# A fused decoder layer: the last stage moved beside the last expert, the first expert rows in five loads, spare products in the last batch, and scatters behind the maxima's transfers

## What is computed

```python
gates = softmax(x_flat @ router_w + router_b)
_, topk_idx = top_k(gates, 2)
pos = cumsum(expert_mask, axis=0) - 1          # place of a row in its expert
buf[e, pos] = x_flat[row]                      # rows beyond the capacity are dropped
h = gelu(einsum('ecd,edh->ech', buf, w1) + b1)
out = einsum('ech,ehd->ecd', h, w2) + b2
y = sum over a row's experts of weight * out[expert, pos]
result = layernorm(x + y)
```

## Time and profile before

| | us |
|---|---|
| median of 3 runs | 2276.23 |
| lowest, highest | 2272.47, 2283.42 |
| the profiled execution, its own time | 2272.46 |
| its span | 2270.7 |
| PE busy in it | 2169.6 (96%) |
| DVE, ACT, Pool busy | 1180.0, 1007.8, 648.9 |

### The profile page before, as it was taken

How to read it: one execution, slowest core, us unless ns; L and a number is a source line. 1 busy time by engine, 2 the same in 40 slices (tenths; PEclk the granted TensorE clock), 3 DMA queues, 4 the chain that set the end, 5 groups by cost and what they waited for, 6 DMA issues and landing times. The chain is left out here.

```text
span 2270.7 us, 48602 instructions
## 1 busy us (share of the span) xinstructions
PE 2169.6 (96%) x18846; PEld 1509.7 (66%) x18846; DVE 1180.0 (52%) x2458; ACT 1007.8 (44%) x1538; POOL 648.9 (29%) x1001
## 2 busy tenths in 40 slices
PE   8999999999999999999999999999799999999990
PEld 4566666666666666666666666666478778787780
DVE  3466666766766766667676676764111111111114
ACT  1355555555555555555555555553231222212225
POOL 2112323333233332333323333222312122121223
PEclk6799999999999999999999999998799999999995
DMA  6301111111101111001010010100113331333217
GB/s 181 102 21 30 44 31 49 53 42 51 51 27 31 37 30 29 22 26 33 25 30 22 28 33 24 28 20 14 37 35 84 77 71 32 82 84 77 24 17 303
DMA packets 97667, 115.72 MB, mean 51 GB/s; under 512 B 12097, under 2 KB 91022, under 8 KB 95393
## 3 DMA queue, kind: packets, MB, share of 16 engines
q1 hardware_dynamic: 68112, 82.38, 11.5%
q0 software_dynamic: 17664, 18.35, 5.1%
q10 hardware_dynamic: 11664, 11.88, 1.8%
HBM read 64.53 MB, written 56.05 MB: 53 GB/s over the span
## 5 line engine op out<-in xcount | busy, mean ns | idle before, releaser
L867 DVE TENSOR_REDUCE smax<-ps_s 128x4 f32<-128x1024 f32 x500 | 610.0, 1220 | 352.3 <-PE ps_s L574 286.3
L753 ACT ACTIVATE prob<-ps_e 128x1024 f32<-128x1024 f32 x500 | 512.3, 1025 | 524.5 <-PE ps_e L583 427.4
L574 PE MATMUL ps_s<-stack 17*128 17x256 f32 x4000 | 574.1, 404 | 24.9 <-DVE smax L867 9.8
L583 PE MATMUL ps_e<-stack 18*128 18x256 f32 x4000 | 574.7, 405 | 5.6 <-DMA stack<-nrows 3.9
L574 PEld LDWEIGHTS ps_s<-stack 17*128 17x128 f32 x4000 | 350.6, 186 | 206.6 <-issue 97.7
L583 PEld LDWEIGHTS ps_e<-stack 18*128 18x128 f32 x4000 | 345.7, 186 | 11.4 <-DMA stack<-nrows 5.9
L1543 ACT ACTIVATE hid<-m_ps_h,b_sb 128x320 f32<-128x320 f32 x256 | 135.0, 527 | 415.7 <-PE m_ps_h L1503 411.5
L1503 PE MATMUL m_ps_h<-m_cols,w_sb 128*128 128x320 f32 x1024 | 293.3, 436 | 0.6 <-DVE m_cols L1560 0.6
L1520 PE MATMUL m_ps_o<-w_sb,hid 128*128 128x256 f32 x1280 | 278.9, 379 | 0.0
L1520 PEld LDWEIGHTS m_ps_o<-w_sb,hid 128*128 128x128 f32 x1280 | 243.2, 190 | 34.8
L599 PE MATMUL ps_w<-prob,val 128*32 128x256 f32 x4096 | 257.3, 393 | 1.3 <-ACT prob L753 1.3
(11 more groups left out here) (134 smaller groups left out, 2270.8 us busy)
## 6 DMA issues: line engine op xcount, KB each, us to landing
w_sb<-in_w SPq DMA_DIRECT2D x16, 1024.0 KB, 6.5
slot_rows_dram<-fill ACTq DMA_DIRECT2D x8, 1290.0 KB, 9.7
m_rows<-slot_rows_dram SPq DMA_DIRECT2D x16, 645.0 KB, 4.5
xT<-in_xT SPq DMA_DIRECT2D x32, 256.0 KB, 2.8
ctxT<-in_ctxT SPq DMA_DIRECT2D x32, 256.0 KB, 2.8
x_res<-in_x SPq DMA_DIRECT2D x32, 256.0 KB, 2.9
stack<-nrows SPq DMA_DIRECT2D x512, 2.0 KB
sums_dram<-x SPq DMA_DIRECT2D x32, 256.0 KB
```

What stands on the lines that cost most here:

```text
L574: mm = nc.tensor.matmul(scores[:, p % 2, t, :], stack[X][rows, Q, p // HG, t * P:(t + 1) * P], stack[X][rows, K, p // HG, :], start=True, ...
L583: mm = nc.tensor.matmul(shifted[:, p % 2, t, :], stack[Y][rows, K, h // HG, t * P:(t + 1) * P], stack[Y][rows, Q, h // HG, :], start=True, ...
L753: nc.scalar.activation(prob[:, h:h + 2, :].rearrange("p h s -> p (h s)"), shifted[:, :, :, :].rearrange("p h t s -> p (h t s)"), ACT.Exp, ...
L867: nc.vector.tensor_reduce(max_columns(X, p), scores[:, :, :, :], AX.X, ALU.max)\
```

## The change

Four parts.

1. *The last stage beside the last expert.* SP loads the eight groups of sums once the scatters of chunks 12 and 13 have landed. DVE, Pool and ACT work on the groups between their instructions for chunks 14 and 15: DVE all moments and the normalisation of groups 5 to 7, ACT the normalisation of groups 0 to 4 (22 of 40 tiles after the Gelus of chunk 14, two after each piece of chunk 15, four after the last). The last expert's results are no longer scattered into the sums. Pool gathers the sums of their rows (`l_got`, ten gathers), DVE adds them (`last_sum`), makes their moments and normalises them, and Pool scatters the finished rows over those that SP has written to the output, after all eight writes have landed.
2. *The first expert rows in five loads.* `m_rows` and `spin` are made before the first block (`FirstRows`); the tile `fill`, which held zeros in the first steps, now lies in `m_rows`. SP loads chunk 0 in five transfers, one per tile, at the end of the first block, as soon as it has seen the last scatters land. PE waits for each tile by itself.
3. *Spare products.* 8 in (32, CROSS), 14 in (33, SELF), 50 instead of 45 in (34, CROSS), and 4 at the start of the second block.
4. *Scatters.* In the SELF half step Pool waits for the four transfers of the first half of the maxima before it issues the scatters. For batch 30 the own positions and `place` come before the inverse deviation.

```diff
+            spins_beside_one_stream = {
+                (last + 1, CROSS): (0, (0, 0, 2, 3, 3, 0, 0, 0)), (last + 2, SELF): (2, (2, 2, 3, 2, 0, 2, 1, 2)),
+            }
...
-                     (last + 3, SELF, 3): 2, (last + 3, SELF, 7): 12, (last + 3, CROSS, 7): 45}
+                     (last + 3, SELF, 3): 2, (last + 3, SELF, 7): 12, (last + 3, CROSS, 7): 50}
...
+                    if (i, X) in spins_beside_one_stream:
+                        n, times = spins_beside_one_stream[i, X]
+                        if times[m] and n in held:
+                            steps_of, at_b, at_k = held[n]
+                            pe.wait_ge(steps_of.sem, steps_of.count(at_b, at_k))
+                        keep_warm(times[m], ps_w[:, n, :])
...
                     if there(i - 4) and i - 4 < NB - 2:
+                        if there(bX):
+                            pool.wait_ge(max_in[SELF].sem, max_in[SELF].count(bX, 64))
                         scatter(i - 4)
...
             sp.wait_ge(slots_zero, (E + 1) * 16)
+            sp.wait_ge(gone.sem, gone.count(NB - 1))
+            first_rows.load(sp)
...
+    def load(self, sp):
+        for c in range(CT):
+            sp.dma_start(self.rows[:, 0, c, :], DRAMS.slots[c * P:(c + 1) * P, :]).then_inc(self.come[c], 16)
...
         for u in range(2):
-            sp.wait_ge(sent.sems[u], sent.count(CHUNKS - 2 + u, u))
+            sp.wait_ge(sent.sems[u], sent.count(LAST - 2 + u, u))
...
+        for q in (0, 1, 2, 3, 5, 6, 4, 7):
+            if q < ACT_GROUPS:
+                sp.wait_ge(by_act.sem, by_act.count(q))
+            else:
+                sp.wait_ge(by_dve.sem, by_dve.count(q - ACT_GROUPS))
+            send_group(q)
...
+        fetch(0, 0, CT)
+        fetch(1, 0, 2)
+        group_inverse(0)
+        group_inverse(1)
+        fetch(1, 2, 4)
+        group_inverse(2)
+        fetch(1, 4, CT)
+        for q in range(3, GROUPS):
+            group_inverse(q)
+        last_inverse(0, 0, CT, 2 * CT, 0)
+        pool.wait_ge(c_sent, 16 * GROUPS)
+        place_last(0, 0, CT)
+        last_inverse(1, 0, CT - 1, 2 * (CT - 1), 0)
+        place_last(1, 0, 1)
+        last_inverse(1, CT - 1, CT, 2 * CT, 1)
+        place_last(1, 1, CT)
...
+                if q == CHUNKS - 1:
+                    for n in (22 + 2 * m, 23 + 2 * m):
+                        normalise(n // GT, n % GT)
+            if q == LAST:
+                for n in range(22):
+                    normalise(n // GT, n % GT)
...
+        group_moments(1, 0, GT)
+        group_moments(2, 0, GT // 2)
+        for c in range(CT):
+            last_sum(LAST, 0, last_pe, c)
+            q, part = divmod(5 + c, 2)
+            group_moments(q, part * GT // 2, (part + 1) * GT // 2)
+        for q in range(5, GROUPS):
+            group_moments(q, 0, GT)
+        last_moments(LAST, 0, 0, CT)
+        for q in range(ACT_GROUPS, GROUPS):
+            group_normalised(q)
+        last_normalised(0, 0, CT, 0)
+        dve.wait_ge(noted.sem, noted.count(LAST + 1))
+        for c in range(CT - 1):
+            last_sum(LAST + 1, 1, last_pe, c)
+        last_moments(LAST + 1, 1, 0, CT - 1)
+        last_sum(LAST + 1, 1, last_pe, CT - 1)
+        last_moments(LAST + 1, 1, CT - 1, CT)
+        last_normalised(1, 0, CT - 1, 0)
+        last_normalised(1, CT - 1, CT, 1)
```

More of the change, by code:

```diff
@@ L1456, in store, with fetch @@
                 ).then_inc(sent.sems[u], 16)
-        turns(pool, store)
+        def fetch(u, first, end):
+            if first == 0:
+                pool.wait_ge(noted.sem, noted.count(LAST + u))
+                pool.sem_inc(fence)
+            for c in range(first, end):
+                nc.gpsimd.indirect_dma_start(
+                    out=got[:, u, c, :], out_offset=None, in_=DRAMS.sums[:, :],
+                    in_offset=bass.IndirectOffsetOnAxis(ap=token_of[:, u, c:c + 1], axis=0),
+                    bounds_check=TOKENS + SPARE * P - 1, oob_is_err=False,
+                ).then_inc(fetched[u], 16)
@@ new lines, in last_inverse @@
+        def last_inverse(u, first, end, done, part):
+            pool.wait_ge(l_moments[u].sem, done)
+            pool.sem_inc(fences[0])
+            nc.gpsimd.tensor_scalar(l_veps[:, u, first:end], l_mv[:, u, first:end, 1], EPS, None, ALU.add)\
+              .then_inc(l_inv[u], 1)
+            pool.wait_ge(l_inv[u], 2 * part + 1)
+            pool.sem_inc(fences[0])
+            nc.gpsimd.tensor_tensor(l_rstd[:, u, first:end], l_veps[:, u, first:end], minus_half[:, 0:end - first],
+                                    ALU.pow).then_inc(l_inv[u], 1)
@@ L1532, in _, with normalise @@
     def _(act):
+        def normalise(q, g):
+            if g == 0:
+                act.wait_ge(inv, inverses(q, 4))
+            nc.scalar.activation(out_tile[:, q, g, :], out_tile[:, q, g, :], ACT.Identity, bias=shift[:, q, g:g + 1],
+                                 scale=rstd[:, q, g:g + 1]).then_inc(by_act.sem, 1)
         def emit(q, e, u, pe_):
@@ L1566, in columns, with group_moments @@
             nc.vector.tensor_copy(gate_of[:, u, :], rows[:, u, :, D + 1]).then_inc(noted.sem, 1)
+        def group_moments(q, first, end):
+            if first == 0:
+                dve.wait_ge(come[q], 16)
+            for g in range(first, end):
+                nc.vector.bn_stats(c_stats[:, q, g, :], out_tile[:, q, g, :]).then_inc(moments.sem, 1)
+            if end == GT:
+                dve.wait_ge(moments.sem, moments.count(q, GT))
+                dve.sem_inc(fences[1])
+                for g in range(GT):
+                    nc.vector.bn_aggr(mv[:, q, g, :], c_stats[:, q, g, :]).then_inc(moments.sem, 1)
@@ L1568, in emit, with last_normalised @@
+        def last_normalised(u, first, end, part):
+            dve.wait_ge(l_inv[u], 2 * part + 2)
+            for c in range(first, end):
+                nc.vector.tensor_scalar(res[:, u, c, :], res[:, u, c, :], l_mv[:, u, c, 0:1], l_rstd[:, u, c:c + 1],
+                                        ALU.subtract, ALU.mult).then_inc(l_normed[u], 1)
         def emit(q, e, u, pe_):
-            if not isinstance(q, int) or q + 1 < CHUNKS:
-                columns(q + 1, 1 - u)
+            columns(q + 1, 1 - u)
```

162 lines of the change are left out of this document (113 added, 49 removed).

## The result

The changed kernel takes **2250.3 us** (median of 4 runs, 2247.6 to 2253.6) against 2275.1 for the kernel before beside it: ratio 0.989, 95% interval 0.987 to 0.991. It is faster, but the gain is 25 us where 54 were forecast, and the time lies outside the range (2211 to 2238).

The account below looks back on a forecast made before the run. PE was taken as busy without a break at full clock except at the end, the last attention batch and the experts' start. 2272.5 - 37.2 - 6.2 - 8.9 = 2220.2, plus 2 for scatter: 2222 us, range 2211 to 2238.

Parts of the forecast that it names:

- Scatters behind the maxima: Steady attention loop, 28 batches: Pool waits for SP's four transfers before its four scatters; cost 0, gain 0.
- Cover 7.8 us: cost 0: Steady loop: scatters end at 1044.2 instead of 1038.6, still 7.8 us before Pool's addition at 1051.98, so nothing is lost.
- Slower: the new wait on Pool: Rival, steady loop: maxima over 7.8 us later than reckoned cost 1 us per further us in 28 batches; chance 0.03.
- if the period grows: Sign against the forecast, steady loop: a longer batch; Pool's addition was expected at the same place in an unchanged period.
- Last stage: End of the kernel: loads, moments, normalisations and sends move beside the last expert; -37.2 us (bounds -34 to -40).
- group 7's way to DRAM: Tail of the last stage: group 7 leaves DVE at 2206.8 and is in DRAM about 4 us later, 2210.9.
- Start of the experts: First expert rows: earlier load in five pieces (-3.4) and clock held by spares (-2.8); -6.2 us (bounds -0.5 to -6.5).
- The clock part: Start of the experts: if spares hold the clock, the first 24 hidden products take 6.46 instead of 9.27 us, -2.8.
- Spare products: Last batch of attention: 22 spares beside one stream hold the clock at 2.4 GHz; -8.9 us (bounds 0 or +4).
- the last four: Chances said to lie outside the range: tail shorter 0.06, stage not beside the expert 0.03, slower 0.03, gains eaten 0.02.
- the shorter tail: Rival, end of the kernel: plain placing lands in 2 us and DVE makes no wait; 2213 us, chance 0.06.
- both: Rival: clock not held and a last-expert queue in PE's way together; 2243 us, chance 0.05.

Follow-up runs that it names:

- e2: The kernel before with only Pool's wait for the maxima ahead of the scatters added; 2291.7 us, ratio 1.012 to the kernel before.
- e10: The changed kernel without Pool's wait for the maxima ahead of the scatters, run again on a chip with the pause; 2230.5 us, ratio 0.980 to the kernel before.
- e9: The changed kernel itself run once more, on a chip with the pause; 2250.3 us, ratio 0.989 to the kernel before.
- e18: The changed kernel without Pool's wait for the maxima, as the reference on e17's chip; 2229.6 us, ratio 0.980 to the kernel before.
- e16: The changed kernel without Pool's wait for the maxima, as the reference on the chip of e13 to e15; 2228.8 us, ratio 0.982 to the kernel before.
- e1: The changed kernel without Pool's wait for the maxima ahead of the scatters, all else as changed; 2222.6 us, ratio 0.980 to the kernel before.
- e4: e1 with the four scatters issued half a batch later, behind the additions of the turned parts; 2253.3 us, ratio 0.995 to the kernel before.
- e14: e1 with two of the four scatters of a batch issued, back to back; 2218.7 us, ratio 0.977 to the kernel before.
- e15: e1 with all four scatters, one each at four places of the batch; 2219.1 us, ratio 0.977 to the kernel before.
- e13: e1 with only the first of the four scatters of a batch issued; 2210.3 us, ratio 0.973 to the kernel before.
- e11: e1 with all scatters of attention left out, on a chip with the pause; 2205.4 us, ratio 0.969 to the kernel before.
- e12: e1 with the four scatters replaced by four plain transfers from Pool's queue, on a chip with the pause; 2212.5 us, ratio 0.972 to the kernel before.
- e5: e1 with all scatters of attention left out, on a chip where no pause was seen; 2207.6 us, ratio 0.980 to the kernel before.
- e8: e1 with the first expert rows in one load instead of five, where no pause was seen; 2213.7 us, ratio 0.983 to the kernel before.
- e17: e15 with the scatter behind the turned parts moved next to the one behind the masked keys; 2220.0 us, ratio 0.975 to the kernel before.

## Why the prediction was wrong, step by step

**Scatters behind the maxima: the step that failed.** "Cover 7.8 us: cost 0" is true for Pool and wrong for the kernel. Measured: 27.5 us in the changed kernel, 26.4 us for the wait alone (e2), 0.98 us a batch. The rival "Slower: the new wait on Pool" asked only whether Pool would come late to its addition; it needed maxima over 7.8 us late. They weren't, Pool idled 8.15 us, and still its scatters did harm, through something that the step's accounting had no line for: what a row of indexed scatters does to PE's products and releases. The pause was in the trace of before, in every batch, as releases of 1.1 us; there it fell where PE had twelve products and no semaphore. The wait moved it 6 us, to where PE makes a duo that ACT and DVE wait for and itself soon waits for them. The prediction named the sign that would prove it wrong, "if the period grows", and that is what happened. What in the scatters makes the pause stays open.

**Last stage: right, 2.6 us short of the -37.2.** Chunk 13's last product to the last product of all: 71.4 us (the last product is at 2228.45) against 72.1 forecast; the wait of PE on DVE's bias add of chunk 15 is 1.04 us instead of 2.0, and DVE's first sum of chunk 14 stands 0.04 us behind its bias add, so no gather holds it. (The ten sums take 0.49 us each instead of 0.42.) The rest is the tail: 17.5 us behind the last product instead of 14.1. Two terms were too small. The first is group 7's way to DRAM. DVE's five normalisations of chunk 14 and Pool's first placing:

```profile
2215.74 1.70 DVE L1747 TENSOR_SCALAR m_res<-m_res,l_mv,l_rstd 128x256 f32<-128x256 f32 x5
2217.35 0.41 DVE L1722 TENSOR_TENSOR m_res<-m_ps_o,b_sb 128x256 f32<-128x256 f32 x1
...
2217.82 10.63 PE L1641 MATMUL m_ps_o<-w_sb,hid 128*128 128x256 f32 x48 [1.04 <-DVE m_res L1722]
...
2215.85 6.98 DMA out<-c_rows
...
2223.80 1.11 POOL L1562 DMA_INDIRECT out<-m_res,m_token  x1 [13.44 <-DMA out<-c_rows]
...
2239.54 0.97 POOL L1562 DMA_INDIRECT out<-m_res,m_token  x1 [0.30 <-issue]
```

It took 6.98 us instead of 4 (why, I did not test; SP sends six groups between 2196.36 and 2216.18), and Pool, waiting for all eight groups, began to place its ten tiles only at 2223.80: the last issue came 11.1 us behind the last product instead of 9.9. The second is the end: 6.4 us from the start of the last issue to the end of the span instead of 4.2.

**Start of the experts: -4.5 instead of -6.2.** The clock part came out: the first 24 products take 6.70 us instead of 9.27 (-2.6 of -2.8). The load is issued 2.2 us behind the start of the last scatter, so a scatter lands sooner than the 3.8 I took from an accumulating one, and by that the barrier was 2.0 us of the old 4.2, not 0.4. In the profiled execution the four new spare products then ran at the granted clock 0.50, 1.77 us in front of the transposes, so the hidden products started 10.3 us behind the last scatter. In e10 the four took 1.02 and it was 8.9, which is -3.2 against -3.4 forecast.

**Spare products: right in kind, -5.3 instead of -8.9.** The clock is at 1.00 where it was at 0.50. (The rows give the clock as a share. The 2.4 and 1.2 GHz beside it in the forecast are an estimate: in the changed kernel spare products of 512 columns start 0.216 us apart at 1.00 and 0.427 at 0.50, which is 2.4 and 1.2 columns a ns; that a column takes one cycle no run shows.) The first group with the values takes 1.93 us, as forecast (about 1.9). The last doesn't:

```profile
1619.64 3.44 PE L603 MATMUL ps_w<-prob,val 128*32 128x256 f32 x32 [0.22 <-ACT prob L763]
```

The granted clock is at 0.50 again from 1617 to 1622, and 1.5 of the missing 3.6 us are here; the rest I can't assign. In e9 and e18 the clock had fallen before the spares came (0.59 and 0.61 in the 16 us ahead, 0.89 in the changed kernel as first profiled), and only 1.3 and 0.6 us were left of the gain from the last addition to the last scatter (154.3 and 155.0 against 155.6), though the long stretch had the clock at 1.00 and 0.98 there too. The forecast had no term for what is lost before the spares stand.

Without the failed step the forecast holds: its three mis-sized terms, 2.6 + 1.7 + 3.6 = 7.9 us, make of 2222 about 2230, and e10, e16 and e18 measured 2230.5, 2228.8 and 2229.6 beside a kernel before of 2271 to 2275. That they meet so closely is partly luck: the 28 batches of these three are 6 to 13 us longer than those of the kernel before as profiled, and their starts 3 to 8 us shorter. e1, with 28 batches of the same length as before, took 2222.6, but beside a kernel before of 2265.3. The 0.95 for faster was right, the range was not: its slower end had no room for a step costed at nothing in 28 batches. A mistake of 1 us in a batch is 28 us, more than the whole width of the range. (Nor does the range leave out "the last four" chances, as it says: the shorter tail's 2213 lies inside it, and the 2243 of "both" outside.)

## What to carry to other kernels

- An instruction moved inside a steady loop is judged on every engine that works beside it, not only on its own queue. A cover of 8 us on the moved queue says nothing of PE and those that wait for it; the number of repeats multiplies whatever they lose, so such a step gets its own width in the range.
- Read the release times in the trace (end of the producer to start of the consumer). One that is 1.1 us where its neighbours are 0.15, in each batch at the same place, is a cost that the present order happens to hide, and the first thing that a reordering uncovers.
- Keep rows of indexed scatters where PE has long work that waits for nobody, and don't issue more in a row than must be. Under long products one cost nothing, two 0.15 us and four 0.4 to 0.6; behind the turned parts one cost 0.3; four where PE is soon waited for and waits itself cost 1.4 to 1.6 (e9 and e4 against the batch of 47.04).

## What the runs showed of the hardware

- Behind four indexed scatters from Pool, back to back, PE's releases come late: ACT and DVE start 1.04 to 1.11 us behind the product's end instead of 0.12 to 0.15 (kernel before, e1, e10, e16, e18; medians), 1.44 and 1.47 in e4. As far as the rows tell, ACT and DVE themselves aren't held: in e4 one of them starts 0.7 us before the other, and in the changed kernel DVE goes on with its own steps. Smaller delays stand behind fewer scatters: 0.36 us behind a second one (e14), 0.41 to 0.50 behind a single one at two places of e15, none behind the single one of e13. With none (e11) or with plain transfers (e12) there are none. No late release was seen on the chip of e5 to e8, even with four in a row (e8); those of e1, e9, e16 and e18, and that of the first profiles, have them. What holds PE is open: no row names it. I did not run the changed kernel on the chip without the pause, where by this account it should take 47.05 us a batch too.
- PE can also stop inside a series of products that have no wait between them, for 0.36 us in the batch shown (0.72 in the one behind it), in the changed kernel.
- The granted clock fell to 0.50 for 3.4 us within 3 us of the start of the last scatter's issue, with PE busy for 5.00 of 5 us in the window shown, and that cost 1.2 to 2.3 us in the batch (six of 27 batches in e10, three in e16, two in e18). It also fell behind the second of two scatters, 3 to 4 us behind the start of its issue, in two batches of e14 and four of e17, where releases take about 0.36 us, so the pause is not all of its cause.
- The first 150 us of an execution vary by 8 us (141 to 149) between executions, also of the same code (e1 and e10), with the granted clock from 48 to 100 us at 0.71 and 0.87. The runs of one kernel spread by 2 to 15 us here; how much of that is this stretch, only profiled executions could tell.
